# Attention on one core: the value products of a query tile issued as one group of sixteen

## The reference

```python
h = relu(layernorm((L_norm @ x) @ Wc + bc)); x1 = h + x
q, k, v = (x1 @ Wq), (x1 @ Wk), (x1 @ Wv)          # 4 heads of 32
scores = where(adjacency > 0, q @ k.T / sqrt(32), -1e9)
attn = softmax(scores)
o = (attn @ v) @ Wo + bo
x2 = layernorm(x1 + o)
out = layernorm(x2 + gelu(x2 @ W1 + b1) @ W2 + b2)
```

## Time and profile before

| | |
|---|---|
| three runs | 1069.86, 1075.64, 1075.70 us; median 1075.64 |
| span of the profiled execution | 1062.9 us |
| around the span | 7.0 to 12.8 us, by which of the three runs one takes |
| diffusion and preparation | to 485 us |
| attention | 485 to 953 us |
| MLP | 953 to 1062.9 us |
| TensorE busy over the span | 963.4 us (91%) |

### The profile page before, as it was taken

One profiled execution on the slowest core, in us unless ns is written; L12 is line 12 of the kernel. 1 busy time (PEld: TensorE's weight loads), 2 busy tenths in 40 slices (PEclk: granted clock), 3 DMA queues, 4 the chain that ended last, 5 costly groups with the idle time before them and its releaser, 6 DMA issues. The chain is left out here.

```text
span 1062.9 us, 21229 instructions
## 1 busy us (share of the span) xinstructions
PE 963.4 (91%) x7030; PEld 734.7 (69%) x7030; DVE 642.2 (60%) x2093; ACT 522.0 (49%) x1127; POOL 312.9 (29%) x389
## 2 busy tenths in 40 slices
PE   5998899999999999996899999999999999779861
PEld 4557799999999999784566666666565666456551
DVE  4743333333333335345688878788787888565998
ACT  2232322232222222216777878778787887565530
POOL 0000111111111112131334444434344443026665
PEclk9898999999999999997999999999999999889996
DMA  3000000000000000023344444444343433400111
GB/s 87 1 1 10 11 10 10 10 10 10 20 10 10 10 10 12 1 80 81 99 108 113 119 120 119 119 119 119 93 108 97 114 103 102 99 2 20 40 42 57
DMA packets 47198, 61.18 MB, mean 58 GB/s; under 512 B 4377, under 2 KB 22050, under 8 KB 47138
## 3 DMA queue, kind: packets, MB, share of 16 engines
q1 hardware_dynamic: 47138, 60.51, 21.6%
HBM read 39.53 MB, written 20.97 MB: 57 GB/s over the span
## 5 line engine op out<-in xcount | busy, mean ns | idle before, releaser
L1522 ACT ACTIVATE prob<-prob,low 128x512 f32<-128x512 f32 x256 | 184.2, 719 | 96.8 <-DVE low L1572 96.5
L1572 DVE CUSTOM_DVE_ANT_0 prob<-bank,mask 128x512 f32<-128x512 f32 x256 | 173.4, 686 | 60.9 <-PE bank L1403 60.6
L1416 PE MATMUL bank<-ident,prob 128*128 128x128 f32 x1024 | 170.6, 290 | 1.1 <-ACT probT L1511 1.1
L1416 PEld LDWEIGHTS bank<-ident,prob 128*128 128x128 f32 x1024 | 109.9, 143 | 53.9 <-issue 48.8
L1403 PE MATMUL bank<-k_stack,q_stack 128*128 128x512 f32 x256 | 125.6, 492 | 23.2 <-DMA q_stack<-bounce_k 16.3
L1435 PE MATMUL bank<-probT,v 128*32 128x128 f32 x2048 | 109.6, 287 | 2.0 <-ACT probT L1511 0.8
L1511 ACT ACTIVATE probT<-bank 128x512 f32<-128x512 f32 x176 | 103.0, 585 | 2.1 <-PE bank L1416 0.8
L1058 DVE TENSOR_TENSOR T_lo<-bank,T_hi 128x512 fp32r<-128x512 f32 x48 | 33.0, 688 | 110.5 <-ACT T_hi L896 110.5
L1435 PEld LDWEIGHTS bank<-probT,v 128*32 128x32 f32 x2048 | 40.7, 108 | 77.9 <-issue 60.6
L896 ACT ACTIVATE T_hi<-bank 128x512 fp32r<-128x512 f32 x48 | 28.4, 592 | 132.9 <-PE bank L806 90.9
L594 POOL TENSOR_SCALAR var_eps<-mv 128x4 f32<-128x4 f32 x16 | 3.6, 227 | 293.1 <-DVE mv L1011 293.1
(11 more groups left out here) (232 smaller groups left out, 1927.1 us busy)
## 6 DMA issues: line engine op xcount, KB each, us to landing
k_stack<-bounce_q SPq DMA_DIRECT2D x64, 256.0 KB, 4.4
q_stack<-bounce_k SPq DMA_DIRECT2D x64, 256.0 KB, 4.3
bounce_q<-k_parts SPq DMA_DIRECT2D x16, 512.0 KB, 2.8
bounce_k<-q_parts SPq DMA_DIRECT2D x16, 512.0 KB, 6.0
x_in<-in_x_dram SPq DMA_DIRECT2D x16, 256.0 KB, 2.7
out_dram<-result SPq DMA_DIRECT2D x16, 256.0 KB, 2.2
A<-in_adj_dram SPq DMA_DIRECT2D x4, 256.0 KB, 3.4
W1s<-in_L_gnn_W_dram SPq DMA_DIRECT2D x1, 128.0 KB, 2.4
```

Source lines behind the costliest of these rows:

```text
L1416: last = pe.transpose(psum[2 + u % 2][:, mt * P:(mt + 1) * P], prob[u % RING][:, mt * P:(mt + 1) * P], ident[:, :])
L1522: act.activation(prob[u % RING][:, :], prob[u % RING][:, :], ACT.Exp, bias=low[:, u % TURNED:u % TURNED + 1], scale=-1.0, accum_out=row_su ...
L1572: dve.tensor_tensor_reduce(prob[u % RING][:, :], psum[u % 2][:, :], mask[:, u // HEADS, :], 1.0, 3e38, ALU.add, ALU.min, low[:, u % TURNED ...
```

## The change

`values` now issues all four key tiles of a query tile in one call, sixteen matmuls, instead of four calls of four in four units. It is called in units 3, 7, 11 and 15, as the last thing of the unit: behind that unit's turn, its scores and its extra product, where it stood before them. The lag goes from 8 to 7: the sixteen of a tile stand at the end of unit 4t + 7, where their first four stood at the start of unit 4t + 8. The arithmetic is the same.

```diff
-VALUES_LAG = 8
+VALUES_LAG = 7
...
-                def values(batch, s, t, mt):
-
-                    if mt == 0:
-                        tile_units = range(HEADS * t, HEADS * (t + 1))
...
-                    for head in range(HEADS):
-                        rows = slice(head * HD, (head + 1) * HD)
-                        last = pe.matmul(psum[6 + s][rows, t * P:(t + 1) * P], v[s][:, mt, rows],
...
-                    if mt == NT - 1:
-                        last.then_inc(o_psum, 1)
+                def values(batch, s, t):
+
+                    tile_units = range(HEADS * t, HEADS * (t + 1))
...
+                    for mt in range(NT):
+                        for head in range(HEADS):
+                            rows = slice(head * HD, (head + 1) * HD)
+                            last = pe.matmul(psum[6 + s][rows, t * P:(t + 1) * P], v[s][:, mt, rows],
...
+                    last.then_inc(o_psum, 1)
...
                     for u in range(UNITS):
-                        if u < VALUES_LAG and leaves:
-                            values(e, s, (u + UNITS - VALUES_LAG) // HEADS, u % HEADS)
-                        if u >= VALUES_LAG and attends:
-                            values(a, 1 - s, (u - VALUES_LAG) // HEADS, u % HEADS)
                         if u >= TURN_LAG and attends:
                             turn(a, u - TURN_LAG)
...
                             v_product(pe, one, B_BANK, r)
+                        if u % HEADS == VALUES_LAG % HEADS:
+                            if u < VALUES_LAG and leaves:
+                                values(e, s, (u + UNITS - VALUES_LAG) // HEADS)
+                            if u >= VALUES_LAG and attends:
+                                values(a, 1 - s, (u - VALUES_LAG) // HEADS)
```

More of the change, by code:

```diff
@@ L1418, in turn @@
                     last.then_inc(turned_psum, 1)
-                def values(batch, s, t, mt):
-                    if mt == 0:
-                        tile_units = range(HEADS * t, HEADS * (t + 1))
[L1424 to L1432, removed]
-                    for head in range(HEADS):
-                        rows = slice(head * HD, (head + 1) * HD)
-                        last = pe.matmul(psum[6 + s][rows, t * P:(t + 1) * P], v[s][:, mt, rows],
-                                         probT[(HEADS * t + head) % TURNED][:, mt, :],
-                                         start=mt == 0, stop=mt == NT - 1, skip_group_check=True)
-                    if mt == NT - 1:
-                        last.then_inc(o_psum, 1)
+                def values(batch, s, t):
+                    tile_units = range(HEADS * t, HEADS * (t + 1))
+                    for by_dve in (False, True):
+                        mine = [u for u in tile_units if (u in DVE_COPIES) == by_dve]
+                        if mine:
+                            copy_wait(pe, batch, mine[-1])
+                    if t == 0:
+                        pe.wait_ge(v_copied, batch + 1)
+                        at_least(pe, oT_ready, batch - 1)
+                        pe.wait_ge(k_lo_ready, min(batch + 2, BATCH) if isinstance(batch, int) else batch + 2)
+                    for mt in range(NT):
+                        for head in range(HEADS):
+                            rows = slice(head * HD, (head + 1) * HD)
+                            last = pe.matmul(psum[6 + s][rows, t * P:(t + 1) * P], v[s][:, mt, rows],
+                                             probT[(HEADS * t + head) % TURNED][:, mt, :],
+                                             start=mt == 0, stop=mt == NT - 1, skip_group_check=True)
+                    last.then_inc(o_psum, 1)
                 def round_(r, s, half):
```

## The result

The changed kernel is slower. Its median is 1086.25 us (four runs, 1081.75 to 1088.97) against 1074.36 us for the kernel before (four runs, 1069.86 to 1075.70). The ratio is 1.0133, with a 95% interval of 1.0095 to 1.0171. The forecast was 1071.9 with a range of 1059 to 1082, so the time lies outside it. The prediction gave 0.08 to a loss of more than 1%, which this is by the ratio, though 1086.25 lies just under the 1086.4 that it named for it. Of ten executions of a kernel one was far or slightly above the rest in four of the experiments (e1 1080.06 us, e5 1193.59, e6 5005.85, e8 3114.46); the ratios leave it out, the medians keep it.

The account below looks back on a forecast made before the run. TensorE and the transfers were taken to run level, so most saving becomes waits: -0.6 (leg 2) + 1.5 (first leg) - 9.5 (branch) - 4.2 (tail) + 9.1 (clock) = -3.7 us, from 1075.64 to 1071.9, range 1059 to 1082.

Parts of the forecast that it names:

- What bounds the kernel: From k_lo to the next first scores, TensorE's work and the transfers run level, so TensorE's saving goes into waits.
- leg 2: From k_lo to the next first scores: keeps its length, as the transfers set it; only small waits go, -0.6 us.
- The products: Value products on TensorE: a block costs 1.15 us against 2.00 before, saving 3.4 us a batch, 54 us for 16.
- In the four rounds behind a branch the change helps by a way round: VectorE's 2.17 us idle at its loop branch falls into the wait for transfers: -9.5 us over four rounds.
- the branch is not hidden: Rival: VectorE's branch still costs time in four rounds; the sum loses 5.5 us, giving 1077.4 us; chance 0.1.
- First leg: First scores to k_lo: the block ahead of unit 13's turn delays VectorE, +0.3 us in five rounds, +1.5 in all.
- The clock: TensorE's new idle 2.6 us before first scores halves its clock in half of 14 rounds, delaying k_lo: +9.1 us.
- the clock falls in every round: Rival: TensorE's clock falls each round, a term of 18.2 us, giving 1081.0 us, slower than before; chance 0.2.
- The tail: Behind batch 15's first scores no transfer is waited for, so TensorE's saving counts: -4.2 us, between -2 and -5.5.

Follow-up runs that it names:

- e1: The changed kernel with eight extra matmuls on TensorE just before its wait for the next batch's transfers; median 1073.39 us, ratio 1.0019 to the kernel before.
- e5: The changed kernel with the block of query tile 2 moved from the end of unit 15 to the end of unit 0; 1073.35 us, ratio 1.0016.
- e6: The changed kernel with the block of query tile 3 moved from unit 3 to unit 4, behind the scores of unit 5; 1068.65 us, ratio 0.9973.
- e8: The changed kernel with VectorE's loop over rounds written out, so that it has no branch; 1078.85 us, ratio 1.0065.
- e3: The kernel before, with both writes of a batch issued ahead of all its reads; 1058.76 us, ratio 0.9890.
- e4: The changed kernel with both writes of a batch issued ahead of all its reads; 1041.15 us, ratio 0.9732.
- e7: The changed kernel with lag 8 (blocks one unit later) and both writes ahead of the reads; 1029.85 us, ratio 0.9602.
- e2: The changed kernel with a lag of 8 instead of 7, all four blocks one unit later; 1064.28 us, ratio 0.9938.
- e10: The changed kernel once more, unaltered, beside the kernel before; 1084.02 us, ratio 1.0099 with ten runs.

## Why the prediction was wrong, step by step

**What bounds the kernel: right.** TensorE waits for q_stack in every round, leg 2 keeps its length (18.22 us against 18.33), and e3 with e4 show that two clocks ran level before: a shorter chain alone gives 1.1%, and with the changed order 4.0% of the changed kernel's time.

**The products: right for one unit, too large for a round.** A convolution unit takes 1.38 us from turn to turn (1.37 predicted):

```profile
796.17 0.60 PE L1416 MATMUL bank<-ident,prob 128*128 128x128 f32 x4
...
797.55 0.60 PE L1416 MATMUL bank<-ident,prob 128*128 128x128 f32 x4
```

The block is 1.01 us from its start to the next turn's (785.57 to 786.58; predicted 1.15). TensorE's busy time in a round at full clock falls from 27.11 to 25.26 us, 1.9 where 3.4 were predicted. (From e3 to e4 it falls by 34.0 us in 14 rounds, 2.4 each, but e3's is longer by the half clock of four rounds, and e4's clock never fell.) So the distances were right, and the busy time of a round falls by less than they add up to. Why is open; the ends of matmuls are modelled, and with them the busy time.

**"In the four rounds behind a branch the change helps by a way round": the step that failed most,** with -9.5 us predicted and +0.3 measured. Part of the -9.5 was there for another reason: the leg of 13.46 us at 744.03 holds a fall of the clock (0.50 from 749.5 to 752.9 in the profile of before), and not only a branch. The first half of the step came true: VectorE was done 1.5 us before the scores were issued (753.67 against 755.19), where before it ended behind them. The idle time of 2.17 us was then taken for a fixed price that could be moved into the wait. It is not fixed. The instructions behind a branch come as packets of an instruction queue, which the profile counts on the same 16 DMA engines as those of q_stack; in e8, without the branch, this queue has none at these places. The instruction queue of the changed kernel from 753 to 758 us, and below it that of the kernel before from 743.5 to 747.5 (packets, MB, share of 16 engines' time):

```profile
q14 instruction: 3, 0.02, 2.6%
```

```profile
q14 instruction: 3, 0.02, 2.2%
```

Three packets take 2.6% x 16 x 5 = 2.1 us together now, and took 2.2% x 16 x 4 = 1.4 us. The largest takes 1033 ns at each of the four branches now, and 569 at most before and 551 in e4. This is 0.5 to 0.6 us of the 1.3 to 1.8 by which the gap grew; the packets also start later, the first 0.3 us behind the end of VectorE's last instruction (753.98), where before it started 1.1 us ahead of it (743.50), and what holds them back is not shown. From the end of VectorE's last instruction to the next of any kind were 2.21, 1.98, 1.79 and 1.88 us before and are 3.56, 3.74, 3.57 and 3.30 now. In e3, e4 and e7, where VectorE ends 0.7 us or more behind the last landing, they are 1.45 to 1.80, and in e2, where it ends just ahead of it, 2.74 to 3.22. VectorE resumes 2.1 to 2.2 us behind the last landing now, and 2.1 to 2.4 before: it comes to the branch earlier and leaves it no earlier. In e10, e1, e2, e5 and e6 it is 1.9 to 2.3 us. The rival "the branch is not hidden" had the mechanism, but left the term at -4 us, from products missing in units 1 and 2; +0.3 was measured, and e8, without the branch, is 5.8 us better in these legs. The Trainium skill ("Runtime: NRT & Kernel Launch", section "Instruction fetch mechanics") says that a taken branch can force a DMA fetch of its target before the engine goes on; the rows agree. That the fetch takes longer beside the reads of q_stack is shown by these rows and by e4, in which the compute engines' programs are those of the changed kernel, VectorE comes to the branch behind the last landing, and the gap is 1.45 to 1.51 us.

**First leg: the right sign, the wrong block.** The copy on VectorE comes 2.13 us behind the first scores, as worked out. But the walk stopped at the start of the round and did not follow k_lo back from its own place, where it stands behind a reduce that stands behind the block of unit 3. A first leg of 9.77 us was expected at full clock and 10.50 came; moving that block alone takes off 0.75 (e6). As this holds in all of the ten rounds, where +0.3 us was taken in five, the term was +8.4 us instead of +1.5.

**The clock: the mechanism right, the count wrong, the sum near by luck.** Behind batch 1's the waits were 1.83 to 2.60 us long, mostly shorter than the 2.6 expected, and the clock still fell in 12 of 14 rounds (11 in e10), not in half. A fall costs 0.9 us (11.41 - 10.50), not 1.3. So a term of 9.1 was taken for 14 rounds, and 7.3 us were seen in the ten that show it cleanly: more falls at a smaller price each. By the count the rival "the clock falls in every round", which was to decide from about 10 of the 14 on, came true; its 1081.0 us still held the -9.5 of the branch and the -4.2 of the tail. Behind a branch the clock fell too, but there VectorE was waiting for its instructions, and the leg (12.11 to 12.26 us) is no longer than in e1, where the clock held in two of the four (12.24 and 12.09). The Trainium skill's rule ("TensorE: Matmul & The Clock Gate", section "Loop structure matters more than you think") spoke for every round, with a wait of 8 us in its example; the trace, with waits of 1.8 to 3.9 us, agrees with it in 12 of 14. In e2 and e6, which wait in every round too, it fell in 7 and 5, so the rule gives the direction and not the count.

**The tail: wrong.** Without transfers TensorE's saving was expected to count, 4.2 us. It grew by 2.6 us (1.2 in e10); 1.1 us of this, in both profiles, lie ahead of the last value product, and the rest in the MLP. From 933.03 TensorE is busy for 19.64 of 23.39 us, against 21.47 of 23.03 before: it saves 1.8 us and loses it in waits. Two rows of it, the start of the round and a turn later on:

```profile
933.03 0.80 PE L1403 MATMUL bank<-k_stack,q_stack 128*128 128x512 f32 x1 [4.52 <-DMA q_stack<-bounce_k]
933.75 1.94 PE L1435 MATMUL bank<-probT,v 128*32 128x128 f32 x32
...
944.96 0.63 PE L1416 MATMUL bank<-ident,prob 128*128 128x128 f32 x4 [0.92 <-ACT probT L1511]
```

The round begins at half clock, with a block of 1.94 us in front of the turn; and later a block holds up the scores for 1 us, VectorE and ScalarE run dry, and TensorE waits for their copy. The clock is not the reason for the loss. In e3 and e4 it is 1.00 from batch 15's first scores to the last value product, and this stretch is 28.23 us in e3 and 29.61 in e4: the grouping costs 1.4 us there. With the blocks one unit later (e7, the clock at 1.00 too) it is 26.83, so the place costs 2.8 us and the grouped products are worth 1.4 in their better place. The windows of e3, e4 and e7, with columns as in the earlier trace rows:

```profile
913.92:942.15 28.23, 25.65 (x300) 16.36 (x300) 20.75 (x62) 20.08 (x48) 3.83 (x4) 1.00 0.01 1
896.24:925.85 29.61, 22.68 (x299) 17.45 (x300) 20.50 (x61) 20.41 (x49) 3.82 (x4) 1.00 0.01 1
886.99:913.82 26.83, 22.34 (x300) 17.50 (x300) 20.45 (x62) 20.07 (x48) 3.82 (x4) 1.00 0.01 2
```

## What to carry to other kernels

When an engine is busy for 99% of a round, look whether a transfer lands just before it goes on: if it does, a saving on the engine turns into waits until the transfer starts sooner. Work that is gathered in one block delays whatever a slower chain needs next, so walk back from the instruction that starts the chain (here k_lo, and the reduce ahead of it) and not forward from the place of the edit. Here the order of gains was transfers first, blocks second, branch third; with the transfers mended, the change that had cost 1% was worth 1.6%, and 2.9% with its blocks one unit later (0.9602 / 0.9890).

## What the runs showed of the hardware

- Behind a branch VectorE stood still for 1.45 to 1.80 us where it came to it 0.7 us or more behind the last landing (e3, e4, e7), and for 3.30 to 3.74 us where it came 1.2 us or more ahead of it (the changed kernel; 2.96 to 3.79 in e10); the largest instruction packet took 1033 ns there.
- The clock of TensorE fell to half behind idle stretches of 1.83 to 2.60 us in 11 rounds and held behind two, of 2.52 and 1.84 us. The length of the idle stretch alone does not decide it. With eight more matmuls in the wait, which add 10.8 us to TensorE's busy time over 14 rounds (378.87 - 368.05), it held in 12 of the 14 rounds, and the kernel was about 1% faster.
- A block of sixteen 128 x 32 products takes 1.01 us at full clock, 0.25 for four; at half clock it took 1.94. Four between full-array matmuls lengthened a unit by 0.50 us, twice as much; that the other half is the change from one form to the other is a guess.
- Issuing the second write before waiting for the first shortened a chain of two writes and eight reads by 2.1 us, of 18.2, though its last reads were issued 4.7 us sooner behind k_lo.
